# Identity transposes on TensorE, a head shared by two engines, and a last stage with a buffer for every expert

## What is computed

```
x = x + tanh(g_xattn[0]) * L0_xattn(layernorm(x), ctx, ctx, mask, ...)   # 16 heads of 16
x = x + tanh(g_ffn[0])   * L0_ffn(layernorm(x), ...)    # 8 experts, each takes its 512 best tokens
x = x + tanh(g_xattn[1]) * L1_xattn(layernorm(x), ctx, ...)
x = x + tanh(g_ffn[1])   * L1_ffn(layernorm(x), ...)    # each token goes to its first choice of 8 experts
```

```
Sim = (enc @ w1)[:, None] + (ctx @ w2)[None, :] + (enc * w3) @ ctx.T + b
A = softmax(Sim, axis=keys);            hq = A @ ctx
Batt = softmax(max(Sim, axis=keys));    hc = Batt @ enc
out = concat([enc, hq, enc * hq, enc * hc]) @ W_qv + b_qv
```

## Time and profile before

| | us |
|---|---|
| timed, median of 3 runs (lowest, highest) | 761.59 (760.83, 762.41) |
| the profiled execution, its own time | 757.5 |
| its span, first to last instruction | 755.7 |
| TensorE busy in the span | 662.5 (88%) |
| VectorE, ScalarE, POOL busy | 419.4, 330.5, 260.5 |

### The profile page before, as it was taken

One profiled execution on the slowest core, in us unless ns is written; L12 is line 12 of the kernel. 1 busy time (PEld: TensorE's weight loads), 2 busy tenths in 40 slices (PEclk: granted clock), 3 DMA queues, 4 the chain that ended last, 5 costly groups with the idle time before them and its releaser, 6 DMA issues.

```text
span 755.7 us, 14748 instructions
## 1 busy us (share of the span) xinstructions
PE 662.5 (88%) x5303; PEld 463.6 (61%) x5303; DVE 419.4 (56%) x1290; ACT 330.5 (44%) x703; POOL 260.5 (34%) x377
## 2 busy tenths in 40 slices
PE   5999997999999968649999999996699999993883
PEld 3575654666666645424666666555578888882772
DVE  5653736788888747762122221113268887773563
ACT  2334333888888844333212222221635555510650
POOL 4101101344444431023554444323101334344365
PEclk9999999899999997967999999999699999996997
DMA  8659971577777129702373894316213473122662
GB/s 264 211 169 218 263 190 58 90 149 151 141 157 151 60 94 181 217 25 63 57 166 43 250 259 91 61 22 175 76 57 112 142 250 113 57 85 73 213 224 80
DMA packets 105040, 103.12 MB, mean 136 GB/s; under 512 B 22102, under 2 KB 95321, under 8 KB 104964
## 3 DMA queue, kind: packets, MB, share of 16 engines
q1 hardware_dynamic: 95752, 85.72, 43.8%
q0 software_dynamic: 9216, 16.46, 9.7%
HBM read 60.15 MB, written 42.25 MB: 135 GB/s over the span
## 4 chain that ended last, share of the span: by engine, by line
PE 49%; DVE 3%; ACT 3%; DMA 3%; issue 2%; POOL 2%; POOLq 0%; SPq 0%; ACTq 0%; DVEq 0%
PE pc L1488 10%; PE pc L1465 10%; PE pc L2288 4%; PE pc L2015 3%; PE pc L2008 3%; PE pc L952 3%; PE pc L2053 2%; PE pc L1975 2%; PE pc L2006 2%; PE pc L1484 1%; PE pc L2075 1%; PE pc L1468 1%; PE pc L1452 1%; PE pc L2083 1%; ACT junk_s L1082 1%
## 5 line engine op out<-in xcount | busy, mean ns | idle before, releaser
L618 ACT ACTIVATE probs<-pb,b_key_cols 128x512 f32<-128x512 f32 x128 | 91.8, 765 | 6.9 <-PE pb L788 6.7
L1368 POOL DMA_INDIRECT scratch_resid<-y,k_idx x32 | 54.7, 1708 | 87.8 <-DVE y L1418 87.5
L484 DVE TENSOR_REDUCE neg_max<-pb 128x4 f32<-128x512 f32 x128 | 81.2, 676 | 4.4 <-PE pb L768 3.7
L1436 ACT ACTIVATE mid<-pc,b_up 128x512 f32<-128x512 f32 x40 | 27.5, 687 | 113.9 <-PE pc L1465 113.9
L1465 PE MATMUL pc<-gT,w_up 128*128 128x512 f32 x160 | 73.1, 613 | 0.9 <-DVE gT L1400 0.9
L1488 PE MATMUL pc<-w_dn,mid 128*128 128x256 f32 x320 | 73.3, 384 | 0.0
L1488 PEld LDWEIGHTS pc<-w_dn,mid 128*128 128x128 f32 x320 | 59.5, 190 | 12.7 <-issue 5.3
L1465 PEld LDWEIGHTS pc<-gT,w_up 128*128 128x128 f32 x160 | 31.4, 197 | 38.0 <-issue 37.6
L1418 DVE TENSOR_SCALAR y<-pc,gate 128x256 f32<-128x256 f32 x32 | 15.5, 483 | 65.4 <-PE pc L1488 47.6
L1359 POOL DMA_INDIRECT rows<-scratch_rows,k_idx x32 | 31.2, 975 | 57.4 <-DVE k_idx L1242 48.0
L801 PE MATMUL pb<-probs,v_wide 128*32 128x128 f32 x1024 | 42.7, 283 | 0.3
(11 more groups left out here) (342 smaller groups left out, 1407.4 us busy)
## 6 DMA issues: line engine op xcount, KB each, us to landing
qs<-scratch_qparts SPq DMA_DIRECT2D x48, 128.0 KB, 4.3
ks<-scratch_kparts SPq DMA_DIRECT2D x48, 128.0 KB
w_dn<-in_W_down SPq DMA_DIRECT2D x8, 640.0 KB
scratch_slots<-s_zero SPq DMA_DIRECT2D x1, 4160.0 KB, 18.5
c_in<-in_ctx SPq DMA_DIRECT2D x8, 512.0 KB, 6.9
s_x<-in_x SPq DMA_DIRECT2D x8, 512.0 KB, 7.3
scratch_ctxT<-cT SPq DMA_DIRECT2D x8, 512.0 KB, 6.7
scratch_resid<-s_x SPq DMA_DIRECT2D x16, 256.0 KB, 3.7
```

Of the source, the lines that this page charges most:

```text
L484: V.tensor_reduce(neg_max[:, h:h + 4], ps_s[b][:].rearrange("p (h k) -> p h k", h=4), AX.X, ALU.max, negate=True).then_inc(max_s, 1)
L618: A.activation(probs[2 * u + b][:], ps_st[b][:].rearrange("p (h q) -> p h q", h=4), ACT.Exp, bias=key_cols[:, 1, t:t + 1], scale=key_cols[ ...
L1368: pool.indirect_dma_start(out=T["resid"], out_offset=bass.IndirectOffsetOnAxis(ap=S["idx"][:, e, c:c + 1], axis=0), in_=y[e % 2][:, c, :], ...
```

## The change

- A helper `turn_identity` transposes the identity matrix `times` times into a bank nobody reads. It is called 11 times over before `turn_keys(0)`; 28 at the start of `tables_on_tensor`, behind a new wait for VectorE's first four lookups; 20 before `turn(0)` of stage three, 5 inside it before each of the chunks 1 to 3 (behind the wait for the chunk) and 5 after it; 34 after `gap_on_tensor(1)`, and in step 0 of the cross attention 6 before `similarity(0)`, 14 before `rows_across(0)`, 16 before `keys_across(0)`, 6 before `columns_back(0)`. The 14 at the start of the last stage become 12.
- Head of the cross attention: x of quad 0 comes in two transfers of two tiles; VectorE normalises tiles 2 and 3 of quads 0 and 1 (`first_rows`) and makes the second half of `encW` of quad 0 (`first_keys`), where ScalarE did all. `gap_on_vector(1)` moves from behind `statistics(1)` to between `first_rows(0)` and `first_keys`. ScalarE's `encT` of quad 0 waits for both halves of `encW`.
- Last stage: eight buffers each for rows, weights and biases; SP issues all loads of all experts with no wait between. Rows of expert 0 come in three transfers. The semaphores of experts 4, 5 and of 6, 7 are shared in pairs. VectorE normalises chunks 0 and 1 of expert 1; ScalarE's normalisation goes in pairs of chunks between the turned copies. The indices of expert 0 are made in three steps.

```diff
+def turn_identity(nc, S, bank, times):
+    for _ in range(times):
+        nc.tensor.transpose(bank[:, 0:P], S["ident"][:], S["ident"][:])
...
             pe.wait_ge(made, 6)
+            turn_identity(nc, S, ps[4], 11)
             turn_keys(0)
...
                 pe.wait_ge(xg_s, e * ST + c + 1)
+                if e == 0 and c:
+                    turn_identity(nc, S, ps[7], 5)
...
+        turn_identity(nc, S, ps[7], 20)
         turn(0)
+        turn_identity(nc, S, ps[7], 5)
...
         sp.wait_ge(ffn.added, ffn.all_added)
-        for q in range(3):
+        sp.dma_start(x_in[0][:, 0:2, :], x_t[:, 0:2, :]).then_inc(x_in_s[0], 16)
+        sp.dma_start(x_in[0][:, 2:QUAD, :], x_t[:, 2:QUAD, :]).then_inc(x_half_s, 16)
+        for q in (1, 2):
             load_x(sp, q)
...
             for t in range(QUAD):
+                if (q, t) == (0, 2):
+                    dve.wait_ge(x_half_s, x_half_in)
                 V.bn_stats(stats[:, t, :], x_in[q % 5][:, t, :]).then_inc(st_s, 1)
...
+        def first_rows(q):
+            dve.wait_ge(shift_s, q + 1)
+            for t in (2, 3):
+                V.tensor_scalar(enc[q][:, t, :], x_in[q][:, t, :], rstd[q][:, t:t + 1], shift[q][:, t:t + 1], ALU.mult, ALU.add).then_inc(enc_s, 1)
+
+        def first_keys():
+            dve.wait_ge(te_ps, 1)
+            V.tensor_scalar(encW[:, 1, :], ps_e[1][:], w_sim[:, 2, 1:2], w_sim[:, 1, 1:2], ALU.mult, ALU.add).then_inc(encW_s, 1)
...
+            if s == -1:
+                first_rows(0)
+                gap_on_vector(dve, 1)
+                first_keys()
             if is_quad(s + 2):
                 statistics(s + 2)
-            if s < 0:
-                gap_on_vector(dve, s + 2)
+            if s == FIRST:
+                gap_on_vector(dve, 0)
...
+            if s == 0:
+                first_rows(1)
             if is_quad(s - 1):
                 residual(s - 1, 0)
...
-            for t in range(QUAD):
+            for t in range(QUAD if q > 1 else 2):
                 A.activation(enc[q % 2][:, t, :], x_in[q % 5][:, t, :], ACT.Identity, ...
...
     def tables_on_tensor(pe):
         M = nc.tensor
+        pe.wait_ge(route.found_d, 4)
+        turn_identity(nc, S, ps[0], 28)
         pe.wait_ge(route.found_a, 16)
...
+        idle_turns = {"rows": 34, "keys": 6, "top": 14, "weights": 16, "back": 6}
+        turn_identity(nc, S, ps_hq[0], idle_turns["rows"])
...
-    ST, WARM = CAP // P, 14
+    ST, WARM = CAP // P, 12
...
-    rows, xn = [sb(f"g_rows{i}", [P, ST, ROW1]) for i in range(4)], ...
+    rows, xn = [sb(f"g_rows{i}", [P, ST, ROW1]) for i in range(EXPERTS)], ...
+    w = S["w_1"] + [sb(f"g_w{i}", [P, HALVES, D]) for i in range(4, EXPERTS)]
+    bias = S["b_1"] + [sb(f"g_b{i}", [P, D]) for i in range(4, EXPERTS)]
...
     def weights(sp, e):
-        if e >= 4:
-            sp.wait_ge(y_s, (e - 3) * ST)
...
+        sp.dma_start(rows[0][:, 0:1, :], slots_t[:, 0:1, :]).then_inc(in_s[0], 16)
+        sp.dma_start(rows[0][:, 1:2, :], slots_t[:, 1:2, :]).then_inc(second_s, 16)
+        sp.dma_start(rows[0][:, 2:ST, :], slots_t[:, 2:ST, :]).then_inc(others_s, 16)
+        for e in range(1, 4):
+            sp.dma_start(rows[e][:], slots_t[:, e * ST:(e + 1) * ST, :]).then_inc(in_s[e], 16)
+        for e in range(4, EXPERTS):
+            weights(sp, e)
+            sp.dma_start(rows[e][:], slots_t[:, e * ST:(e + 1) * ST, :]).then_inc(late_s[e // 2 * 2], 16)
...
         for e in range(1, EXPERTS):
             for j in range(2):
+                turned_out(e, j)
+                if e + 1 < EXPERTS:
+                    norm(e + 1, 2 * j, 2 * j + 2)
...
+        chunk(0, 0)
+        norm(1, 0)
+        norm(1, 1)
+        for c in range(1, ST):
             chunk(0, c)
-        index(1)
+        index(1, 0, ST)
```

More of the change, by code:

```diff
@@ L2210, in on_scalar, with norm, turned_out @@
     def on_scalar(act):
[L2211 removed]
+        def norm(e, first, end):
+            loaded(act, e)
+            if e == 1:
+                act.wait_ge(xn_s, ST + first)
             if e >= 3:
                 act.wait_ge(t_ps, ST if e == 3 else turned(e - 3, 1))
[L2214 to L2217 removed]
+            for c in range(first, end):
+                nc.scalar.activation(xn[e % 3][:, c, :], rows[e][:, c, 0:D], ACT.Identity, bias=rows[e][:, c, D:D + 1],
+                                     scale=rows[e][:, c, D + 1:D + 2]).then_inc(xn_s, 1)
+        def turned_out(e, j):
+            act.wait_ge(t_ps, turned(e, j))
+            if e >= 2:
+                act.wait_ge(y_ps, (e - 2) * ST + 2 * j + 2)
+            nc.scalar.activation(rT[e % 2][:, :, 2 * j * P:2 * (j + 1) * P], ps[e % 2 * 2 + j][:].rearrange("p (h t) -> p h t", h=HALVES),
+                                 ACT.Copy).then_inc(rT_s, 1)
         for c in range(ST):
@@ new lines, in on_scalar, with norm, index @@
+                if e + 1 < EXPERTS:
+                    norm(e + 1, 2 * j, 2 * j + 2)
+    def on_vector(dve):
+        def norm(e, c):
+            if e == 0:
+                dve.wait_ge(*((in_s[0], 48), (second_s, 16), (others_s, others_in), (others_s, others_in))[c])
+            else:
+                loaded(dve, e)
+            nc.vector.tensor_scalar(xn[e][:, c, :], rows[e][:, c, 0:D], rows[e][:, c, D + 1:D + 2], rows[e][:, c, D:D + 1],
+                                    ALU.mult, ALU.add).then_inc(xn_s, 1)
+        def index(e, first, end):
+            if e:
+                loaded(dve, e)
@@ L2318, in on_tensor @@
         pe.wait_ge(bidir.sent_s, 16 * TILES)
[L2319 to L2320 removed]
+        turn_identity(nc, S, ps[7], WARM)
         turn_chunk(0)
```

102 lines of the change are left out of this document (46 added, 56 removed).

## The result

The changed kernel runs in 755.07 us (median of 4 executions, 754.41 to 756.49) against 761.49 (760.83 to 762.41): a ratio of 0.9903, interval 0.9885 to 0.9921. The medians are 6.4 us apart. The ratio is an estimate of its own and not the quotient of the two medians, which is 0.9916; put on 761.5 it says 7.4 us. The forecast was 15.3 us, 746.3, with 754 as its upper end.

The account below looks back on a forecast made before the run. TensorE was taken to bound the middle of the stages, leaving gains only at three heads and the POOL-bound end. 1.4 + 2.9 + 5.8 + 5.2 = 15.3 us off the median 761.59 gave 746.3; range 742 to 754.

Parts of the forecast that it names:

- term of the last stage (5.2): Last stage: shared normalisations and early loads remove POOL's extra idle before two writes, winning 5.2 us.
- "0.6" for x in halves: Head of the cross attention: two of four statistics run before x's second half is in, winning 0.6 us (0 to 0.7).
- front (1.4): Kernel start: 11 identity transposes raise the clock, so the eight products of the keys run faster; 1.4 us (0 to 3.8).
- "keeps the gain" behind the heads: Steady cross attention: from 548.60 on TensorE is full again and carries the heads' gain on, losing nothing.
- I take this distance to stay: Base of the sum: the timed median, 761.59, stays 4.1 us above the profiled execution, 757.5.
- Head of the choice, 2.9: Head of expert choice: identity transposes keep the clock up, `up(0)` wins 3.3 us, one pair is 0.3 late; net 2.9.
- Head of the cross attention, 5.8: Head of the cross attention: sharing, halves and full clock win 6.2 us in all, taken as 5.8; below 3.0.
- its own sign: Last stage, sign of being right: POOL's last write starts some 40.5 us after its first, with no idle over 0.6.
- POOL runs back to back from the second write: Last stage: with both pauses gone POOL writes chunks without idle from its second write on, winning 5.2 us.
- the loads stand in the way: Rival, last stage: 18 transfers at once fill the DMA, so the stage gains only 0 to 1 us; 751.0, chance 0.12.
- The clock did fall between the groups: Rival: pauses between transpose groups drop the clock, costing 1.0 us in choice, 3.0 in cross attention; 751.0, chance 0.20.
- identity transposes are useless: Rival, choice and cross attention: identity transposes do not raise the clock and are only work; slower, 764.9 us, chance 0.04.

Follow-up runs that it names:

- `old_last_stage`: The changed kernel with the last stage of the kernel before: 749.54 us, ratio 0.9936 to the kernel before.
- `before_third`: The kernel before, unchanged, traced a third time on the chip that the changed kernel got there: 763.37 us, ratio 0.999.
- `last_stage_only`: The kernel before with nothing but the new last stage of the change: 751.44 us, ratio 0.9947.
- `before_again`: The kernel before, unchanged, run again for a second trace: 755.96 us, ratio 1.000.

## Why the prediction was wrong

In short, four steps failed. The term of the last stage (5.2) was too large even where nothing disturbs it (3.3 to 4.1), and gave -1.3 in the trace of the change. "0.6" for x in halves was a loss of 1.0, because an instruction fetch moved onto the load. The front (1.4) gave 0.3, since the clock rose early in half of the traces only. And "keeps the gain" behind the heads failed, by 2.8 between the two traces of the result and by 0.5 to 1.2 between like traces. Where no update is late the two parts sum to 9 to 10 us, not 15.3, so the late updates are not the whole of the error.

**The base.** "I take this distance to stay": 757.5 against a median of 761.59. It does not. The profiled execution of before had no late update; where the kernel before has them it takes 763 to 765. I read an unusually good execution as a fixed offset, and planned the sum on a trace that lacked late updates. The other three executions took 760.8 to 762.4, between the 755 of the chips without and the 764 of those with them. Whether they had them no trace shows.

**Front, 1.4: 0.3.** The transposes can raise the clock (3.67 us for the keys in 7 of 14 traces with them, never under 5.2 in the six without), but not in each execution: in the first trace of the change the clock rose at 11.0, in `old_last_stage` at 6.6, with the same 11 transposes at the same time. The rule stands in the Trainium skill ("TensorE: Matmul & The Clock Gate", Part 1: The HAM clock gate): how many instructions run cold differs from run to run with the phase that the clock gate is in when the kernel starts; these traces agree. And in six of the seven where it rose early it fell again at 16 to 17, so that the eight products at L704 took 5.0 to 5.4 (5.40 before). Those products end at 22.1 on the mean of the 14 traces with the transposes, and at 22.6 on that of the six without: 0.5. With 7 of 14 the term should have been about half of 1.4.

**Head of the choice, 2.9: 1.2.** The step is right where nothing is late: from the end of L704's eight to the load of x 493.7 and 493.9 us in two such traces, against 496.1 and 496.6: 2.4 and 2.7. In the first trace of the change ScalarE heard of the first product of `up(0)` late, and `up(0)` took 10.3 us instead of 8.8, of which 1.2 is TensorE's wait.

**Head of the cross attention, 5.8: 5.1.** The number is near by two errors that offset each other. Sharing, the turn, `similarity(0)` and the queries came as worked out, and `row_max` did become VectorE's. The step that failed is "two of four statistics run before the second half is in: 0.6". The half is worth 1.1 (2.8 instead of 3.95). But the change puts 79 transposes, and so 158 instructions (each is a weight load and a product), on TensorE ahead of the load of x, and with them the fetch of the next block moved from 544.9 to 520.9, onto the transfer of x: 4.4 to 4.9 us in all nine traces with the halves and a fetch there, 5.45 for the whole x, 2.6 to 2.9 in all five halved ones without. With the fetch out of the way this head takes 22.0 to 22.5 us, where before took 28.9 to 29.2: 6.4 to 7.2 won, more than the 5.8 forecast and its 6.2 in all. The Trainium skill ("Runtime: NRT & Kernel Launch", Instruction fetch mechanics) has TensorE refill in blocks of 16 KB and calls the cost of a crossing mostly hidden; the blocks are in the traces, the cost here was some 1.9 us. I had counted what the transposes cost on TensorE and not what they move.

**Behind the head, 0: -2.8.** "From 548.60 on TensorE is full again and keeps the gain" was true of the trace that I had. With late updates VectorE starts `d_hc_row` 0.6 later in a quad, its list runs into `elementwise`, and TensorE, with no slack, ends the quad 0.5 later, 0.35 of it in front of the transposes of the result. This is a loss of late updates and not of the change: the kernel before has it too (18.2 us a quad in `before_third`), so against a like trace it is 0.5 to 1.2 and not 2.8. Where no update is late the quads keep to 17.64 in the changed kernel's heads too.

**Last stage, 5.2: -1.3.** Measured alone it gave 4.1 and 3.3, with 40.7 and 41.2 us of writes. The sum had taken the writes from 44.65 to 39.5, every step at 1.27, while its own sign said 40.5. Undisturbed they took 40.7. And 1.4 of the 5.1 counted as pauses came from a fall of the clock that another trace of the same kernel does not have; the pause of 1.92 before the write at 730.57, put down to rows loaded late, is 0.53 there, with late rows as well. "POOL runs back to back from the second write" needs TensorE's news in time; with late updates there are pauses of up to 2.0 us in the first trace of the change and 4.0 in the others, and the leads of TensorE that the change makes are no use. The rival "the loads stand in the way" had the right size (0 to 1) and, as far as the runs show, the wrong cause: with the same 18 loads and no late update (`last_stage_only`) the gain is there, and ScalarE waits once for rows, 0.7 us; with direct writes once, 2.6 us.

**The rivals.** The clock did fall between the groups, which the prediction had named as a sign of being wrong. In the head of the choice it did so in 13 of the 14 traces with the transposes (335.3 to 338.7 in the first), but it was back before `up(0)` in all of them, so the price was small, and 8 instead of 28 transposes behind the lookups do as well. In the cross attention it fell once between the groups (526.5, 0.4 us of `similarity(0)`) and once behind them (549, 1.7 us). That identity transposes are useless is refuted: in seven traces the clock rose at 5.7 to 7.0 us, when TensorE had run nothing but transposes; the keys' 3.67; `up(0)` at 8.8 instead of 10.2 to 11.9; and 3.1 us lost without those of the cross attention. The rule of the Trainium skill for transposes ("TensorE: Matmul & The Clock Gate", Part 4: PE-mode transpose), cited with that rival, does not hold for these in fp32.

**The range.** 742 to 754 left out "the mechanism is right and half is lost on the way". Measured ratios of the change are 0.9903, 0.9886, 0.9883 and 0.9895; the parts alone sum to 0.988. Put on 761.5 they are 752 to 754, at the upper end of the range; the median of the changed kernel, 755.07, lies 1.1 above it. That the ratios come so near is luck: the upper end was made for other failures than those that came.

## What to carry to other kernels

A profiled execution that lies well off its kernel's median is not a base with an offset: look for what it lacks, and take a second trace. When two traces are compared, see that both have the same disturbance; here the steady part seemed to lose 2.8 us and lost 0.5 to 1.2. Count the instructions that an edit adds to an engine also as fetches: a 16 KB block lands somewhere, and here it cost 1.9 us on an exposed transfer. The last of a transfer's 16 landing events shows it. Filler work that holds the clock up pays in pauses of known place, less at the start of a kernel, where it worked in 7 traces of 14.

## What the runs showed of the hardware

- TensorE's semaphore updates can reach the other engines 0.5 to 4 us late, while its own instructions go on; in the last stage one came out per 1.44 us (709.50, 710.93, 712.38, 713.84, 715.28), and then several within 0.2. In the same stretches semaphore events of VectorE and ScalarE are late or missing in the trace (26 of 55 and 24 of 42 have none within 0.45 us from 700 to 745 in the first trace of the change, none of 63 and 47 in that of before). It happened in every trace of three comparisons (two chips), whatever the kernel, and in none of two (two other chips), at the same places each time, and stopped in the last stage where GpSimd's writes were not indirect. Why some chips or executions have it is open.
- Whether this is there when nothing is recorded is open, as all executions timed here have their clock recorded. The Trainium skill ("NOTIFIC — the notification-queue block", 7.1 Overflow) says that the block that takes the records can, in one of its three modes, hold back the engine that makes them. No run here shows that this is the cause.
- Between the chips without and with late updates the kernel before differs by 8 to 10 us (755.0 and 755.6 against 763.8 to 765.1). Of the 9.9 between the two traces `before_again` and `before_third` 3.0 lie between `similarity(1)` and the last stage's first load and 5.0 behind that, the places of the late updates. The changed kernel differs by some 10 (745.5 to 746 by the sum of its parts against 756), which is why the ratio hardly depends on the late updates.
- A fetch of 16 KB of TensorE's instructions beside a load holds up one of the 16 landing steps of the load: 4.4 to 4.9 us instead of 2.5 to 2.9, while the other 15 come by 2.4 to 2.9 in both cases.
